# Weighted values of an attention kernel in one block of 512 queries per group, in place of two of 256

## What is computed

```python
attn = jnp.einsum('bhqd,bhkd->bhqk', query, key) / scale
attn = jax.nn.softmax(attn, axis=-1)
out = jnp.einsum('bhqk,bhkd->bhqd', attn, value)
```

## Time and profile before

| what | value |
| --- | --- |
| median of 3 runs | 3534.08 us (3529.81 to 3535.11) |
| profiled execution, its own time | 3549.16 us |
| profiled execution, span | 3547.4 us |
| mean granted TensorE clock over the span | 0.962 |
| TensorE, VectorE, ScalarE busy | 93%, 83%, 69% of the span |

### The profile page before, as it was taken

The page is one execution under the profiler, slowest core; times in us unless marked ns, Lnnn a source line. Parts: engine busy times, 40 slices in busy tenths (PEclk is TensorE's granted clock), DMA queues, the critical chain, the costliest instruction groups (busy, mean ns, idle before and its releaser), DMA issues. The chain is left out here.

```text
span 3547.4 us, 67855 instructions
## 1 busy us (share of the span) xinstructions
PE 3290.1 (93%) x27520; PEld 1410.3 (40%) x27520; DVE 2956.7 (83%) x3192; ACT 2443.5 (69%) x4514; POOL 656.9 (19%) x871
## 2 busy tenths in 40 slices
PE   7995999999999999999999999999999997774998
PEld 3441333333333333333333333333333333563665
DVE  5776899999999999999999999999999992675222
ACT  3440788888888888888888888888888887000211
POOL 7871000000000000000000000000000000455664
PEclk9996899999999999999999999999999999776999
DMA  6885112020212111111203020211211100567553
GB/s 203 268 255 122 36 33 62 14 64 18 62 25 51 36 40 39 42 40 36 62 14 63 19 62 23 52 37 39 39 42 37 39 14 24 175 198 201 172 168 92
DMA packets 239160, 267.60 MB, mean 75 GB/s; under 512 B 50587, under 2 KB 170948, under 8 KB 235496
## 3 DMA queue, kind: packets, MB, share of 16 engines
q1 hardware_dynamic: 223488, 233.77, 25.0%
q0 software_dynamic: 15360, 29.50, 2.9%
HBM read 159.56 MB, written 111.88 MB: 77 GB/s over the span
## 5 line engine op out<-in xcount | busy, mean ns | idle before, releaser
L858 DVE TENSOR_REDUCE max_parts<-ps_m 128x2 f32<-128x1024 f32 x2048 | 2495.1, 1224 | 140.3 <-PE ps_m L714 125.6
L843 ACT ACTIVATE probs<-ps_s 128x512 f32<-128x512 f32 x4096 | 2215.5, 596 | 293.1 <-PE ps_s L745 212.8
L714 PE MATMUL ps_m<-keys,queries 48*128 48x512 f32 x4096 | 1510.6, 454 | 43.8 <-DMA queries<-halves_q 29.5
L745 PE MATMUL ps_s<-queries,keys 51*128 51x512 f32 x4096 | 1507.6, 451 | 40.8 <-ACT probs L843 37.4
L762 PE MATMUL ps_o<-probs,vals 128*32 128x256 f32 x16384 | 1309.5, 391 | 0.0
L745 PEld LDWEIGHTS ps_s<-queries,keys 51*128 51x128 f32 x4096 | 610.2, 185 | 890.6 <-issue 817.7
L714 PEld LDWEIGHTS ps_m<-keys,queries 48*128 48x128 f32 x4096 | 603.8, 187 | 91.4 <-issue 55.8
L762 PEld LDWEIGHTS ps_o<-probs,vals 128*32 128x32 f32 x16384 | 322.8, 108 | 741.3 <-issue 738.1
L678 POOL TENSOR_TENSOR heads_out<-weighted,recip_rows 128x512 f32<-128x512 f32 x64 | 82.2, 1285 | 2252.1 <-DMA recip_rows<-recip_rows_dram 2252.1
L1553 DVE TENSOR_TENSOR hidden<-ps_u,silu 128x320 f32<-128x320 f32 x64 | 31.4, 491 | 149.5 <-PE ps_u L1489 70.4
L1532 ACT ACTIVATE silu<-ps_g 128x320 f32<-128x320 f32 x64 | 28.0, 437 | 165.4 <-PE ps_g L1489 136.4
(11 more groups left out here) (104 smaller groups left out, 1785.2 us busy)
## 6 DMA issues: line engine op xcount, KB each, us to landing
rows<-rows_c SPq DMA_DIRECT2D x16, 1032.0 KB
vext<-val SPq DMA_DIRECT2D x64, 256.0 KB, 4.7
halves_q<-parts SPq DMA_DIRECT2D x64, 256.0 KB
halves_k<-parts SPq DMA_DIRECT2D x64, 256.0 KB
keys<-halves_k SPq DMA_DIRECT2D x32, 512.0 KB
queries<-halves_q SPq DMA_DIRECT2D x128, 128.0 KB
vals<-vext SPq DMA_DIRECT2D x32, 512.0 KB
recip_rows<-recip_rows_dram SPq DMA_DIRECT2D x64, 256.0 KB
```

The costliest lines, as they stand in the source:

```text
L714: mm = pe.matmul(ps_m[m % 2][:, h, :], queries_r[rows, par, qt, p, t * P:(t + 1) * P], keys_r[rows, par, p, c * 512:(c + 1) * 512], start= ...
L745: pe.matmul(ps_s[bank][:], keys_r[rows, par, p, k * P:(k + 1) * P], queries_r[rows, par, qt, p, :], start=True, stop=True).then_inc(scores ...
L843: act.activation(probs[:, n % RING, :], ps_s[bank][:], ACT.Exp, scale=SCALE).then_inc(probs_ok[bank], 1)
L858: dve.tensor_reduce(max_parts[:, lu % 2, :, p, t, c], ps_m[m % 2][:], AX.X, ALU.max).then_inc(maxima_ok[m % 2], 1)
```

## The change

`weigh` loses its argument for the half. It is called once in a group, behind all four scores and all four maximum matmuls, and each of its four matmuls covers 512 queries in place of 256. The wait for the exponentials of the weighed group is the same. `pv_ok` is signalled once in a group, as before.

```diff
-                def weigh(step, n, at, half):
+                def weigh(step, n, at):
...
-                    cols = slice(half * (CH // 2), (half + 1) * (CH // 2))
-                    if half == 0:
-                        pe.wait_ge(probs_ok[bank], step * PER_BANK[bank] + at[1][n + QUAD - 1] + 1)
-                    if k == 0 and half == 0:
+                    pe.wait_ge(probs_ok[bank], step * PER_BANK[bank] + at[1][n + QUAD - 1] + 1)
+                    if k == 0:
...
                     for j in range(QUAD):
-                        mm = pe.matmul(ps_o[32 * j:32 * j + 32, cols], vals[:, par, k, VW * j:VW * (j + 1)],
-                                       probs[:, (n + j) % RING, cols], start=k == 0 and half == 0, stop=k == KT - 1 and half == 1)
-                    if half:
-                        mm.then_inc(pv_ok[n // QUAD % SLOTS_PV], 1)
+                        mm = pe.matmul(ps_o[32 * j:32 * j + 32, :], vals[:, par, k, VW * j:VW * (j + 1)],
+                                       probs[:, (n + j) % RING, :], start=k == 0, stop=k == KT - 1)
+                    mm.then_inc(pv_ok[n // QUAD % SLOTS_PV], 1)
...
                             score(step, i + 1, at, first)
-                            if n >= LAG * QUAD:
-                                weigh(step, n - LAG * QUAD, at, half)
-                            elif not first:
-                                weigh(step - 1, TILES + n - LAG * QUAD, PLACES[0], half)
+                        if n >= LAG * QUAD:
+                            weigh(step, n - LAG * QUAD, at)
+                        elif not first:
+                            weigh(step - 1, TILES + n - LAG * QUAD, PLACES[0])
```

More of the change, by code:

```diff
@@ L807, in _ @@
                 for n in range(TILES - LAG * QUAD, TILES, QUAD):
-                    for half in range(2):
-                        weigh(STEPS - 1, n, PLACES[1], half)
+                    weigh(STEPS - 1, n, PLACES[1])
             @block.scalar
```

## The result

The changed kernel takes 3728.16 us (median; 3718.45 to 3731.75) against 3532.48 for the kernel before in the same comparison: a ratio of 1.055, 95% interval 1.0528 to 1.0572. That is 196 us slower. The forecast was slower by 147 us, 3681, with a range up to 3720: the sign and the loop behind it hold, the size does not, and the time lies 8 us outside the range.

What follows compares the result with a forecast made beforehand. TensorE's order was taken to set the pace, VectorE's floor 1% below; the change makes a latency loop. Ordinary groups 130 us, plus 4, 1, 3 and 9, gave 147 us: 3534 to 3681 us, range 3600 to 3720.

Steps and rivals of the forecast that it cites:

- The loop: Attention groups: fourth score waits for the first's exponential to free its bank; 2.61 us a group against 2.48, 130 us.
- The block at 1.00 us: Attention stage: merged weighted-value block of four 512-column matmuls takes 1.00 us, against 1.14 for today's two blocks.
- The sum of the stage: Attention stage: ordinary, turning, copy and last groups together add 147 us, with nothing for the clock.
- Turning groups: Attention groups with the turn of a unit's maxima: 3.19 us against 3.05, 1 us beyond the ordinary growth.
- groups behind a copy: Attention groups after a copy of the weighted sums: 3.68 us against 3.51, 3 us beyond the ordinary growth.
- rival 4: Attention stage: TensorE's pause before the fourth score lowers the clock in a tenth of groups; 173 us on top, 3850; chance 0.04.
- the likeliest case: Attention stage: the latency loop sets the pace, 2.575 to 2.645 us a group, 3645 to 3715 us; chance 0.79.
- a clock under 1.00: Sign for the next profile, attention stage: would mean slower as forecast, but for a wrong reason; no size.
- The last groups: Last 20 attention groups, without maxima: go from 2.18 to 2.61 us a group, adding 9 us.
- VectorE's floor of 2.45: Attention groups: VectorE's two reductions, 2 x 1.226 us, allow no group under 2.45 us.
- The rival at 3507 to 3524: Attention stage: fourth score finds its bank free, groups of 2.45 to 2.47 us, 10 to 27 us less; chance 0.06.
- VectorE's idle time: Sign for the next profile, attention stage: VectorE idle 0.16 us before each group's first reduction, some 160 us more.

Runs made afterwards that it cites:

- experiment 3: Changed kernel with the 512-column block issued between the second and third score of a group instead of behind the fourth: 3620.27 us, ratio 1.0239.
- experiment 5: Changed kernel with 384 of 512 columns in each weighted-value matmul, leaving out a quarter of the queries: 3611.15 us, ratio 1.0214.
- experiment 7: Changed kernel with one of two maximum matmuls of a piece left out and a fourth score bank in the freed memory: 3355.05 us, ratio 0.9489.
- experiment 8: Kernel before with both its 256-column blocks moved behind the fourth score, not merged: 3715.7 us, ratio 1.051.
- experiment 1: Changed kernel with ScalarE's copy of the weighted sums two exponentials (half a group) later: 3632.07 us, ratio 1.0275.
- experiment 9: Changed kernel with the later copy of the weighted sums and extra unread maximum matmuls in the tail together: 3612.85 us, ratio 1.0212.
- experiment 2: Kernel before with ScalarE's copy of the weighted sums two exponentials (half a group) later: 3481.47 us, ratio 0.9836.
- experiment 4: Changed kernel with two extra, unread maximum matmuls a half group in the tail groups that have no maxima: 3707.59 us, ratio 1.0481.
- experiment 6: Changed kernel, three score banks, with one of two maximum matmuls of a piece left out and the other read twice: 3921.48 us, ratio 1.1029.

## Why the prediction was wrong in size

- **The loop: right.** 2.613 forecast, 2.607 measured. Experiments 3, 5, 7 and 8 tell it from its rivals: position in the group makes no difference, block length counts one to one, a fourth bank opens it, the width of an instruction is nothing.
- **The block at 1.00 us: right**, and so is the saving of 0.14 against two separate blocks. It lies in the changes between scores and weighted values: experiment 8 keeps the two narrow blocks and saves as much. The Trainium skill's page "TensorEngine Tiling (Array Packing)", section Key Properties, says that a change of the tiling mode drains TensorE; the 0.14 us agrees with that, though no run tells a drain from another fixed cost of a block. The time saved was not on the path that sets the pace.
- **The sum of the stage: nearly right.** 143 us outside the low clock, 147 forecast. Turning groups 3.20 (3.19), groups behind a copy 3.68 (3.68).
- **The step that failed: the cost of the clock, rival 4, which the sum left at nothing.** It was given 0.04 on the ground that "waits of 1 us at 63 copies leave the clock at 1.00 throughout". This carried a row of the old pattern to a new one. A clock term for some of the copy groups and the tail, not for a tenth of all groups, should have been added to the likeliest case. By the prediction's own sign, "a clock under 1.00", part of its reason was wrong: the stage had 0.98.
- **What the traces show in its place**, each of one execution: in the steady part the clock falls only where the stall at the copy and the pause before every fourth score are both there. The stall without that pause (the kernel before, experiment 7) gave no dip, the pause without the stall (experiments 1, 3 and 9) none, neither (experiment 2) none; both together gave 17 in the changed kernel, 18 in experiment 4, 8 in experiment 8, and with less work 21 in experiment 5 and 39 in experiment 6, each of them 1.5 to 4 us after the start of a copy. In the changed kernel, with its tail at the low level, this is 48 us of the stage's 191, and it is what puts 3728 outside 3600 to 3720. The Trainium skill's page "TensorE: Matmul & The Clock Gate", section A second HAM failure mode, tells of short idle times between groups of matmuls, frequent enough to make the clock go to and fro. The 17 dips agree with it; experiments 1, 3 and 9 do not show it, though TensorE paused in every group: their clock stayed at 1.00 up to the tail.
- **The last groups.** "The loop has no maxima in it, so these too go to 2.61: 9 us" was 0.43 us a group; 12 of them ran at the low clock and took 3.85 to 4.07, 17 us more.
- **VectorE's floor of 2.45: wrong, without effect on the sum.** It was read from the length of a record; two reductions with their input ready take 2.36 us, and a group of 2.395 (experiment 5) lies below it. The rival at 3507 to 3524 was worked out with it: by its own formula a free loop would be at (2.49 + 2.36)/2 = 2.43 us, an estimate, since no run has a free loop with all maxima. VectorE's idle time, forecast to grow by some 160 us, grew by 219 (121.2 to 340.5 from 373 to 2990 us) for the same reason.
- **The parts that no run settles:** why 17 of the copies lower the clock and the others do not, though the pattern behind each copy is the same; and what decides on the tail, which is low in the changed kernel and in experiment 1, and at 1.00 in experiments 3 and 8.

## What to carry to other kernels

Before instructions are collected into a longer run, look at what they stood between. Here a block of matmuls between the second and third score covered the time that ScalarE needs to free a bank; with it moved, three banks for a burst of four became a loop through two engines, and a saving on TensorE turned into a loss. Write down the loop that crosses engines (load, exponential, release, block) and compare it with the pace, as one compares an engine's busy time.

A pause that costs nothing by itself can still cost the clock when it meets another, as the copy's stall and the new pause did here; when a change adds pauses to TensorE at its higher clock, give the clock a term of its own.

## What the runs showed that was not expected

- Two reductions of VectorE that both have their input ready overlap: records of 1.22 us each, but 2.36 us for two and 4.62 for four, so that their starts lie 1.13 to 1.14 apart. In the kernel before, nearly every one starts 0.04 us after the matmul that it waits for, and they looked like 1.226 back to back.
- TensorE with less to do can take longer: without half of its maximum matmuls the changed kernel went from 3728 to 3914 us, with 769 us of the stage at the low clock, and with extra matmuls in the tail it went from 3728 to 3708.
- The group at the low clock takes 4.06 to 4.07 us against 2.61: loads, scores and block all take longer (0.79 in place of 0.50 for a score).
